# An attention block with a slotted post-phase: two idle slots fewer after the first layer norm, and a softmax reciprocal that reads PSUM

## The reference

```python
q = split(x @ Wq + bq); k = split(x @ Wk + bk); v = split(x @ Wv + bv)
pattern = einsum('bhid,bhjd->bhij', k, q) / sqrt(64)
out = einsum('bhis,bhid->bhsd', softmax(pattern, axis=-2), v)
x = layernorm(x + out.reshape(b, s, 1024) @ Wo + bo)
h = gelu(x @ w1 + b1)
x = layernorm(x + h @ w2 + b2)
```

## Time and profile before

| | us |
|---|---|
| three runs shown | 4639.85, 4823.27, 5073.20 (median 4823.27) |
| the profiled execution | 4646.33 |
| span of its slowest core (core 7) | 4644.6 |
| spans of the other cores | 4618.3 to 4641.7 |
| busy: TensorE matmuls / ScalarE / VectorE | 3595.7 / 2307.3 / 1491.9 |
| granted TensorE clock, mean of core 7 | 0.905 |

### The profile page before, as it was taken

The page is one execution under the profiler, slowest core; times in us unless marked ns, Lnnn a source line. Parts: engine busy times, 40 slices in busy tenths (PEclk is TensorE's granted clock), DMA queues, the critical chain, the costliest instruction groups (busy, mean ns, idle before and its releaser), DMA issues.

```text
span 4644.6 us, 57786 instructions; the slowest of 8 cores (4618.3 to 4644.6 us)
## 1 busy us (share of the span) xinstructions
PE 3595.7 (77%) x19264; PEld 1206.9 (26%) x19264; DVE 1491.9 (32%) x1942; ACT 2307.3 (50%) x2191; POOL 193.7 (4%) x344
## 2 busy tenths in 40 slices
PE   5365697787797789778877888788878887888756
PEld 2122242222232223222222222222222222222222
DVE  1133341115223422342234223332333232424343
ACT  0000004885557555755566556565666556655610
POOL 0011100000000000000001000000000000000000
PEclk9677798999999999989999999899989999999977
DMA  8766512113432343223413341234222322232233
GB/s 170 180 158 159 131 64 96 55 55 94 107 78 78 89 110 79 78 84 85 108 60 94 86 111 64 84 87 111 73 84 80 92 81 95 81 89 82 63 83 77
DMA packets 746247, 433.76 MB, mean 93 GB/s; under 512 B 679269, under 2 KB 695781, under 8 KB 728553
## 3 DMA queue, kind: packets, MB, share of 16 engines
q1 hardware_dynamic: 706714, 237.12, 20.7%
q0 software_dynamic: 39248, 192.96, 14.0%
HBM read 377.59 MB, written 77.59 MB: 98 GB/s over the span
## 4 chain that ended last, share of the span: by engine, by line
PE 60%; ACT 16%; DMA 9%; DVE 7%; issue 6%; POOL 1%; ACTq 0%; SPq 0%; DVEq 0%; POOLq 0%
ACT es_sb L814 13%; PE ps_o L824 11%; PE ps_s L801 10%; PE ps_d L836 7%; PE ps_w L714 5%; PE ps_g L714 5%; PE ps_w L670 5%; PE ps_g L670 5%; PE psq L318 3%; PE psq L422 2%; ACT h_sb L688 2%; PE psv L345 2%; DMA xt_f<-xtf_b 2%; DMA wcast<-w 2%; DMA y<-out_sb 1%
## 5 line engine op out<-in xcount | busy, mean ns | idle before, releaser
L814 ACT ACTIVATE es_sb<-ps_s 128x1024 bf16<-128x1024 f32 x2048 | 2097.4, 1024 | 1488.4 <-PE ps_s L801 1339.5
L824 PE MATMUL ps_o<-es_sb,v_sb 128*64 128x512 bf16 x4096 | 858.1, 408 | 478.4 <-ACT es_sb L814 437.5
L801 PE MATMUL ps_s<-q_sb,k_sb 64*128 64x512 bf16 x4096 | 814.1, 400 | 106.9 <-DMA q_sb<-q_scr 85.0
L836 PE MATMUL ps_d<-es_sb,ones 128*64 128x512 bf16 x4096 | 836.9, 391 | 0.0
L824 PEld LDWEIGHTS ps_o<-es_sb,v_sb 128*64 128x64 bf16 x4096 | 258.5, 107 | 1121.7 <-issue 1119.5
L801 PEld LDWEIGHTS ps_s<-q_sb,k_sb 64*128 64x128 bf16 x4096 | 192.6, 93 | 974.4 <-issue 974.4
L865 DVE COPY dD_sb<-ps_d 128x512 f32<-128x512 f32 x64 | 44.3, 692 | 791.9 <-PE ps_d L836 789.7
L670 PE MATMUL ps_w<-h1b_sb,w_sb 128*128 128x512 bf16 x1024 | 256.7, 396 | 27.2 <-DVE h1b_sb L602 19.0
L278 ACT COPY xtf_b<-pst 128x512 f32<-128x512 f32 x64 | 37.5, 587 | 477.5 <-PE pst L270 280.0
L836 PEld LDWEIGHTS ps_d<-es_sb,ones 128*64 128x64 bf16 x4096 | 258.9, 111 | 2.2
L714 PE MATMUL ps_w<-h_sb,w_sb 128*128 128x512 bf16 x1024 | 252.5, 398 | 8.5 <-ACT h_sb L688 8.5
(11 more groups left out here) (94 smaller groups left out, 2395.7 us busy)
## 6 DMA issues: line engine op xcount, KB each, us to landing
k_sb<-k_scr POOLq DMA_DIRECT2D x64, 1024.0 KB, 5.2
v_sb<-v_scr POOLq DMA_DIRECT2D x64, 1024.0 KB, 7.3
w_sb<-w_scr SPq DMA_DIRECT2D x256, 256.0 KB, 3.0
w_sb<-w_scr SPq DMA_DIRECT2D x128, 512.0 KB, 4.3
xnat<-x SPq DMA_DIRECT2D x8, 2048.0 KB, 10.4
xt_f<-xtf_b SPq DMA_DIRECT2D x64, 256.0 KB, 2.3
w_scr<-wcast SPq DMA_DIRECT2D x64, 256.0 KB, 3.7
wo_sb<-wo_scr SPq DMA_DIRECT2D x64, 256.0 KB, 3.7
```

The lines of the kernel that those rows point to most:

```text
L801: fn = lambda e, p=p, b=b, kc=kc, hh=hh: e.matmul(ps_s[kc % 2][:, hh * 512:(hh + 1) * 512], k_sb[b][hh * 64:(hh + 1) * 64, kc * 128:(kc + ...
L814: "act", lambda e, kc=kc, esb=esb: e.activation(es_sb[esb][:], ps_s[kc % 2][:], AF.Exp, scale=SCALE))
L824: tr.op("pe", lambda e, b=b, kc=kc, esb=esb, hh=hh: e.matmul(ps_o[hh * 64:(hh + 1) * 64, :], v_sb[b][:, kc * 128 + hh * 64: kc * 128 + (hh ...
L836: fn = lambda e, kc=kc, esb=esb, hh=hh: e.matmul(ps_d[hh * 64:(hh + 1) * 64, :], ones64[:], es_sb[esb][:, hh * 512:(hh + 1) * 512], start= ...
```

## The change

Two of the four empty `yield`s between layer norm 1 and the FFN go. The copy of ps_d to SBUF goes: the reciprocal reads PSUM itself. The reciprocal now stands before the copy of ps_o, whose number is still `norm_done`. dD_sb is not used any more.

```diff
             yield from emit_ln_tail(y1_sb, h1f_sb, h1b_sb, st1)
-            yield
-            yield
             yield
             yield
             v_ln1 = ln_app
@@
                 free_k[b] = vmm
                 free_v[b] = vmm
                 tr.wait("dve", pe, vmm)
-                tr.op("dve", lambda e: e.tensor_copy(dD_sb[:], ps_d[:]))
+                tr.op("dve", lambda e: e.reciprocal(r_sb[:], ps_d[:]))
                 norm_done = tr.op("dve", lambda e: e.tensor_copy(oO_sb[:], ps_o[:]))
-                tr.op("dve", lambda e: e.reciprocal(r_sb[:], dD_sb[:]))
                 pcol = p * 512
```

## The result

| | before | changed |
|---|---|---|
| median of 10 runs | 4702.02 us (4634.70 to 5073.20) | 4763.54 us (4753.06 to 5133.85) |
| profiled execution | 4646.33 us | 4757.10 us |
| spans of the 8 cores | 4618.3 to 4644.6 us | 4724.2 to 4755.3 us |
| granted clock, by core | 0.903 to 0.907 | 0.889 to 0.894 |

The changed kernel is slower: ratio 1.0259, 95% interval 1.0242 to 1.0276. Some runs of either kernel are several per cent longer because one half of the chip gets a lower clock for a while; the ratios here leave such runs out, the medians do not.

A forecast was written before the change was run, and what follows sets the result against it. TensorE led the last chain (60%), with VectorE's place in it decisive. Stage 0's 28.4 us, seven later stages' 87.5 and -0.8 for the last post-phase sum to 115 on 4646.33: 4761 us, +2.5%, range 4700 to 4940.

The forecast's parts named there:

- The main step: Pair ends: reciprocal before norm_done moves the next pair's pv from T+1.86 to T+4.52 (T: last denom's end), +2.66 us.
- the forecast stands at its level: Forecast time: 115 us added to the profiled execution, 4646.33, giving 4761; on the median it would be 4938.
- pair 5: Interval holding the end of pair 4, stages 1 to 7: forecast -8.0 us; that end alone +0.8 a stage.
- free ends: Ends of pairs without post-phase matmul groups behind them: 2.66 us wait plus 1.40 clock, 4.06 each; 85.2 for 21.
- pair 2: Interval with pair 1's end (+3.3 a stage) and first Gelu (-3.45), stages 1 to 7: forecast -1.1 us.
- phase A and the tail: Before the last post-phase TensorE waits for the whole normalisation, forecast 0.8 us shorter: -0.8.
- Rival 1: Free ends: the clock holds in the 4-us pauses, so only 66 us, 4712, +1.4%; chance 0.22.
- Pair 1: Interval with pair 0's end, layer norm wait (+3.75 a stage) and two moved-in FFN groups: forecast 44.6 us.
- Rival 2: Second Gelu, end of pair 2: clock stays low through two chunks, +3 to +5 a stage, about 4790; chance 0.15.
- Rival 3: The 14 Gelu pauses shrink by more than the ends grow: faster or equal, 4640; chance 0.03.
- Rival 4: Reciprocal slower from PSUM by a full read, 0.69 us at 28 to 35 ends: 4783; chance 0.05.
- The cover named for the end of pair 2: Second Gelu hides the normalisation at pair 2's end: 0 us; without that cover 1.9.

The follow-up runs named there:

- e2: Kernel before with only the reciprocal edit (reads PSUM, stands before the copy of ps_o), four empty slots kept: ratio 1.0375, +168 us by the spans.
- e4: Changed kernel with the copy of ps_d kept, reciprocal reading SBUF, still before the copy of ps_o: ratio 1.0341, +157 us by the spans against before.
- e1: Kernel before with only the two empty slots behind layer norm 1 taken out, normalisation unchanged: ratio 1.0029, +8 us by the spans.
- e3: Changed kernel plus 14 unread matmuls in the pause behind each free end: ratio 1.0220, +88 us by the spans against before.
- e6: Kernel before with FFN groups issued together under both Gelus, plus two empty yields behind each store's: ratio 0.9861 against before.
- e8: Kernel before with two slots taken out inside layer norm 1, the four behind it kept: ratio 1.0028 against before.
- e9: Kernel before with one slot taken out inside layer norm 1 and one behind its broadcast, two kept before Ln: ratio 0.9967 in its second run.

## Why the prediction was right, and where it was not

**What was right.** The forecast on the profiled execution was 4646.33 + 115, +2.5%; measured are 4757.10, +111 us, and a ratio of 1.0259. Of its own signs: `pv` at T+4.47 (4.52 put down), released by the copy of ps_o; reciprocal 3.36 us (3.35 to 3.45); stage 0's pairs 41.2 to 42.1 us (41 to 42); first Gelu pause 7.66 (7.6); second Gelu, `pv` at T+18.6 (18); FFN1's group at T+14.7 to 15.3, behind the cast (T+14.75), though TensorE hardly waits for the cast. The main step, an instruction moved in front of a number that TensorE waits for, is shown by e2 and e4, most plainly by e4 against e1.

**What was wrong: the level of the stated time.** The step that failed is "the forecast stands at its level". The profile's +115 us was put on the profiled execution, 4646.33, and the result named as a time, 4761, beside a median of 4823.27. Read against that median, the one given for before, 4761 is a decrease of 1.3%, while the text forecasts an increase. The prediction saw the 3.8% between the two and used them only to stretch its range. The runs showed an increase: further runs put the median of before at 4702.02 and that of the changed kernel at 4763.54, with a ratio of 1.0259. That the 4761 lies 3 us from the changed kernel's median does not make the step sound. The ratio is what the working gave: 1.025, and it should have been stated so.

**The terms.** That the sum of 115 came within 5 us of the 110 by the mean spans is in part luck: pair 5 came out 10 us above its term, and free ends, pair 2 and the noise of phase A and the tail 15 below theirs.

- Free ends, 85.2 us for 21: measured 78.7. The wait was 2.5 to 2.6 (2.66 put down), the clock's share 1.2 to 1.3 (1.4). Rival 1, a clock that holds, is refuted by the changed kernel, where it fell behind all 168 ends, and by e3: it took useless matmuls to make it hold.
- Pair 1, 44.6: measured 45.7. That the late `pv` and the layer norm wait lie side by side is shown by e1 and e2, which cost 64.2 and 26.4 there. That the clock's term lies inside the wait is shown by e3, where this pair costs the same and the wait comes out.
- Pair 2, -1.1: measured -4.5. The Gelu gains 3.9 a stage in e1 (3.45 put down), the end of pair 1 costs 3.8 in e2 (3.3). Together that is -0.5 over seven stages; the other 4 us of gain I can't place.
- Pair 5, -8.0: measured +1.9, the largest miss, 1.4 us a stage. 0.55 of it: the broadcast's two copies, two chunks in front of the end now, still hold VectorE at T (in stage 4, T = 2889.96, normalisation from T+0.76, so `pv` at T+5.06 and not 4.52; the mean over cores and stages is 5.07). 0.8: from that `pv` to the end of the pair it takes so much longer than before, 2.5 us in stage 1 and between -0.3 and 1.2 in the others. The prediction put this at nothing, since a moved group was to save in its old slot what it costs in its new one; with the slots alone (e1) it is 0.6 a stage, with the reciprocal alone (e2) 0.3, so most of it belongs to the slots. The rest, 0.06, is that `pv` before stood at T+5.61 on the mean and not at 5.67. Why the pair's body is longer stays open; the stores lie in it.

```profile
2889.92 0.69 DVE L591 COPY mrb_sb<-ps_g 128x512 f32<-128x512 f32 x1
...
2890.72 3.36 DVE L863 RECIPROCAL r_sb<-ps_d 128x512 f32<-128x512 f32 x1
...
2895.02 0.64 PE L822 MATMUL ps_o<-es_sb,v_sb 128*64 128x512 bf16 x2 [4.09 <-DVE oO_sb L864]
```

- Phase A and the tail, -0.8: measured -5.7, of which phase A is -3.0. Phase A is the same in all these kernels, and in the others it lies between 3.0 us under the kernel before and 6.6 over it (e6). So I take most of this term for noise of single executions; in the sum it hides half of pair 5's miss.

Rival 2, a bad second Gelu, got 0.15: pair 3 shows 1.4 us, not 21 to 35. Rival 3, Gelu pauses that pay for everything, is bounded by e1: 27 us in pair 2, and none in pair 3. Rival 4, a slow reciprocal from PSUM: 4 ns, not 690. The cover named for the end of pair 2 was real: with the slots restored it costs 2.3 us (1.9 put down).

## What to carry to other kernels

A dependency names an instruction, but what the waiting engine pays is everything queued in front of that instruction: put first, on the releasing engine, only what frees the buffer, and the long arithmetic after it, even at the price of one more copy. Two edits that each delay the same engine at the same place don't add up: in pair 1 they cost 64 and 26 us alone and 46 together. Price them together, or the attribution is wrong by much (here 66 of 110 us). And when moving work by slots, look at which engine's in-order queue its next step waits in: layer norm moved two slots cost once TensorE (e1), once ScalarE and through it TensorE (e8), and only the third placing gained (e9, 0.9967).

## What the hardware showed that I had not expected

A matmul nobody reads can shorten the run. Behind a pause of 3.9 us at a pair's end the granted clock fell every time, at a cost of 1.2 to 1.3 us each; with 14 idle matmuls in the pause it stayed at 1.00, and by the spans 22 us came back. The Trainium skill says of matmul loops with a recurring wait that the clock is lost in each round (TensorE: Matmul & The Clock Gate, HAM oscillation); the trace agrees, 168 times in 168. A reciprocal of 128x512 takes 3357 ns from PSUM and 3353 from SBUF. The Trainium skill's table (VectorE: DVE Perf Modes, the TRN2 errata) gives a PSUM source 62 cycles more, by my estimate 65 ns; for this instruction the measurement shows 4.
